# Eight VectorE lo parts a block: five to an accumulating DMA, three tiles to whole fp32 matmuls

## The reference, cut to what matters

```python
e = stack([tbl_f[ids[:, f]] for f in range(39)])          # (1024, 39, 16), x0
xk = x0
for idx, (W, b) in enumerate(params):                     # W: (39, fields of xk, 128)
    z = relu(einsum('bhd,bkd,hks->bsd', x0, xk, W) + b)
    xk, direct = z[:, :64], z[:, 64:]                     # the last layer: all of z is direct
logit = sum(concatenate(direct, axis=1), axis=-1)
h = relu(concat([logit, dense_ctx]) @ W_top1 + b_top1)
h = relu(h @ W_top2 + b_top2)
y = h @ W_top3
```

## Time and profile before

| | |
|---|---|
| median of 3 runs | 1450.75 us (1449.77 to 1451.19) |
| the profiled execution's own time | 1451.21 us |
| its span, first to last instruction | 1449.1 us |
| mean granted TensorE clock | 0.991 |
| VectorE busy | 1325.9 us, 92% |
| TensorE busy (ends modelled) | 1262.3 us, 87% |
| GpSimd busy | 1233.7 us, 85% |
| ScalarE busy | 638.6 us, 44% |
| DMA: read from HBM, written | 193.17 MB, 12.78 MB |

### The profile page before, as it was taken

How to read it: one execution, slowest core, us unless ns; L and a number is a source line. 1 busy time by engine, 2 the same in 40 slices (tenths; PEclk the granted TensorE clock), 3 DMA queues, 4 the chain that set the end, 5 groups by cost and what they waited for, 6 DMA issues and landing times.

```text
span 1449.1 us, 15741 instructions
## 1 busy us (share of the span) xinstructions
PE 1262.3 (87%) x4040; PEld 730.6 (50%) x4040; DVE 1325.9 (92%) x959; ACT 638.6 (44%) x640; POOL 1233.7 (85%) x655
## 2 busy tenths in 40 slices
PE   0378989999898999989899998989999898999899
PEld 0244545545454555545455554545555554655555
DVE  1389999999999999999999999999999999999872
ACT  1135434454544435454453545444453535535443
POOL 6788989899898989989898998989899896857571
PEclk9989999999999999999999999999999999999999
DMA  4852708154270906327090633618062351806000
GB/s 108 292 178 55 275 6 289 37 198 132 69 260 7 314 10 205 125 79 250 13 313 5 225 105 93 236 25 304 2 228 102 122 206 33 293 1 220 0 0 1
DMA packets 81243, 196.26 MB, mean 135 GB/s; under 512 B 23983, under 2 KB 35342, under 8 KB 81193
## 3 DMA queue, kind: packets, MB, share of 16 engines
q1 hardware_dynamic: 70953, 193.14, 38.8%
q0 software_dynamic: 10240, 2.64, 1.7%
HBM read 193.17 MB, written 12.78 MB: 142 GB/s over the span
## 4 chain that ended last, share of the span: by engine, by line
POOL 58%; issue 22%; PE 10%; DVE 6%; DMA 1%; ACT 1%; POOLq 0%; SPq 0%; DVEq 0%; ACTq 0%
POOL lo L453 29%; POOL emb L443 28%; PE acc L819 8%; DVE prod L716 4%; DVE lo L729 1%; POOL block_idx L432 1%; ACT hi L585 1%; DVE logit L764 0%; POOL pairs_r L473 0%; DMA x_tiles<-x_rows 0%; DVE hi L726 0%; DMA x_rows<-x_rows 0%; PE xk L873 0%; PE acc L873 0%; PE acc L900 0%
## 5 line engine op out<-in xcount | busy, mean ns | idle before, releaser
L453 POOL TENSOR_TENSOR lo<-prod,hi 128x1024 fp32r<-128x1024 f32 (+1 forms) x304 | 758.4, 2500 | 117.0 <-ACT hi L585 113.3
L585 ACT ACTIVATE hi<-prod 128x1024 fp32r<-128x1024 f32 (+1 forms) x464 | 488.1, 1058 | 729.2 <-DVE prod L716 628.4
L716 DVE TENSOR_TENSOR prod<-x_tiles,xk 128x1024 f32<-128x1024 f32 x640 | 740.7, 1212 | 49.2 <-PE acc L819 30.3
L819 PE MATMUL acc<-prod,wfull 128*128 128x512 f32 (+2 forms) x1152 | 549.4, 600 | 1.1 <-DVE prod L716 0.9
L443 POOL DMA_INDIRECT emb<-table,block_idx x320 | 444.3, 1389 | 67.2 <-issue 60.9
L819 PE MATMUL acc<-lo,whi 128*128 128x512 f32 (+1 forms) x864 | 329.7, 466 | 112.8 <-POOL lo L453 92.9
L819 PE MATMUL acc<-hi,whi 128*128 128x512 f32 (+1 forms) x928 | 384.8, 420 | 32.6 <-ACT hi L585 32.4
L819 PE MATMUL acc<-hi,wlo 128*128 128x512 f32 (+2 forms) x928 | 364.7, 398 | 0.0
L819 PEld LDWEIGHTS acc<-lo,whi 128*128 128x128 f32 (+1 forms) x864 | 145.6, 189 | 323.0 <-POOL lo L453 245.8
L819 PEld LDWEIGHTS acc<-prod,wfull 128*128 128x128 f32 (+2 forms) x1152 | 219.9, 191 | 168.5 <-issue 141.3
L729 DVE TENSOR_TENSOR lo<-prod,hi 128x1024 fp32r<-128x1024 f32 (+1 forms) x128 | 276.5, 2160 | 1.1 <-ACT hi L585 1.1
(11 more groups left out here) (62 smaller groups left out, 129.6 us busy)
## 6 DMA issues: line engine op xcount, KB each, us to landing
x_tiles<-x_rows SPq DMA_DIRECT2D x304, 512.0 KB, 9.4
x_rows<-x_rows SPq DMA_DIRECT2D x16, 624.0 KB
x_tiles<-x_rows SPq DMA_DIRECT2D x32, 256.0 KB, 10.4
x_stack<-x_rows SPq DMA_DIRECT2D x48, 156.0 KB
emb<-table,block_idx POOLq DMA_INDIRECT x320, 3.4
x_rows<-x0T SPq DMA_DIRECT2D x64, 32.0 KB, 1.5
x_tiles<-w SPq DMA_DIRECT2D x1, 832.0 KB, 9.3
x_tiles<-w SPq DMA_DIRECT2D x1, 768.0 KB, 6.4
```

What stands on the lines that cost most here:

```text
L453: nc.gpsimd.tensor_tensor(lo[0:r, product_slot(j), :], prod[0:r, product_slot(j), :], hi[0:r, part_slot(j), :].bitcast(f32), ALU.subtract) ...
L585: nc.scalar.activation(hi[0:r, part_slot(j), :], prod[0:r, product_slot(j), :], ACT.Copy).then_inc(hi_ready, 1)
L716: nc.vector.tensor_tensor(prod[0:r, product_slot(j), :], in0, in1, ALU.mult).then_inc(product_ready, 1)
L819: mm = nc.tensor.matmul(z[:, c], w[0:r], part[0:r, c], start=first and i == 0, stop=last and i == len(weights) - 1)
```

## The change

`KINDS` has no D any more. In layer 0 both D tiles become F; in layer 1 the last one does; the other five, tiles 2 and 7 of layer 1 and 2, 7 and 17 of layer 2, become a new kind A. An A tile's lo part isn't subtracted by an engine. ScalarE copies the product a second time, times -1 and rounded, into one of two slots of a new tile `negative`. GpSimd issues a DMA that adds the product from `prod` onto it. TensorE waits for that DMA's own semaphore and multiplies `negative` as the lo part. GpSimd's list has the A tiles among its G tiles, so the gathers are spread over 10, 12 and 2 places. The order of tiles, the slots of products and the loads stay. To make room, `base_sb`, used at the start only, lies where `x0_stack` is.

```diff
-KINDS = ["GFDGDFF", "GFDGF" * 2 + "GFHGF" + "GFDGF", "GGDGF" + "GFDGF" + "GFHGF" + "GFDGF"]
+KINDS = ["GFFGFFF", "GFAGF" * 2 + "GFHGF" + "GFFGF", "GGAGF" + "GFAGF" + "GFHGF" + "GFAGF"]
...
-PRODS, PARTS = 6, 4
+PRODS, PARTS, NEGATIVES = 6, 4, 2
...
+SUMMED = [j for j, k in enumerate(KIND) if k == "A"]
+def negative_slot(j):
+    return SUMMED.index(j) % NEGATIVES
+def negative_before(n, j):
+    return next(i for i in earlier(n, j) if i <= -6 or KIND[i] == "A" and negative_slot(i % STEP) == negative_slot(j))
...
-        base_sb = sb("base_sb", [128, BLOCKS * PAIRS], i32)
+        negative = sb("negative", [128, NEGATIVES, COLS], f32r)
+        base_sb = nc.alloc_sbuf_tensor_at("base_sb", [128, BLOCKS * PAIRS], i32, offset=stack_at)
+        negative_ready = sem("negative_ready")
+        lo_summed = [sem(f"lo_summed{a}") for a in range(len(SUMMED))]
...
GpSimd:
+            def sum_lo(n, j):
+                pool.wait_ge(negative_ready, reached(n, j, "A"))
+                pool.nop(nofuse=True)
+                pool.dma_start(out=negative[:, negative_slot(j), :], in_=prod[:, product_slot(j), :],
+                               accum_op=ALU.add).then_inc(lo_summed[SUMMED.index(j)], 16)
...
-                at, tiles = (L0, L1, L2)[l], [t for t, k in enumerate(KINDS[l]) if k == "G"]
+                at, tiles = (L0, L1, L2)[l], [t for t, k in enumerate(KINDS[l]) if k in "GA"]
...
-                    subtract(n, at + t)
+                    if KINDS[l][t] == "G":
+                        subtract(n, at + t)
+                    else:
+                        sum_lo(n, at + t)
...
ScalarE, in round_hi, behind the hi part:
+                        if KIND[j] == "A":
+                            act.wait_ge(tile_used, reached(n, negative_before(n, j), "FDGHA"))
+                            nc.scalar.activation(negative[:, negative_slot(j), :], prod[:, product_slot(j), :],
+                                                 ACT.Copy, scale=-1.0).then_inc(negative_ready, 1)
...
TensorE, in lo_part:
-                    if KIND[j] in "DH":
+                    if KIND[j] == "A":
+                        part = negative[:, negative_slot(j), :]
+                        pe.wait_ge(lo_summed[SUMMED.index(j)], 16 * (n + 1))
+                    elif KIND[j] in "DH":
```

More of the change, by code:

```diff
@@ L81 @@
 KIND = [KINDS[l][t] for l, t in ORDER]
+SUMMED = [j for j, k in enumerate(KIND) if k == "A"]
+assert not any(L0 <= j < L2 for j in SUMMED)
 def rows(l, t):
@@ L398, in step @@
                     for t in range(REST):
-                        sp.wait_ge(product_ready, reached(n, L2 + t, "FDGH"))
+                        sp.wait_ge(product_ready, reached(n, L2 + t, "FDGHA"))
                         sp.nop(nofuse=True)
@@ L413, in step @@
                 elif not past_end(n, 1):
-                    sp.wait_ge(product_ready, reached(n, STEP - 1, "FDGH"))
+                    sp.wait_ge(product_ready, reached(n, STEP - 1, "FDGHA"))
                     load_top()
@@ L580, in round_hi @@
                         r = rows(*ORDER[j])
-                        act.wait_ge(product_ready, reached(n, j, "FDGH"))
+                        act.wait_ge(product_ready, reached(n, j, "FDGHA"))
                         if not is_step(n, PROLOGUE) or SPLITS[0].index(ORDER[j][1]) >= PARTS:
-                            act.wait_ge(tile_used, reached(n, parts_before(n, j), "FDGH"))
+                            act.wait_ge(tile_used, reached(n, parts_before(n, j), "FDGHA"))
                         nc.scalar.activation(hi[0:r, part_slot(j), :], prod[0:r, product_slot(j), :],
                                              ACT.Copy).then_inc(hi_ready, 1)
+                        if KIND[j] == "A":
+                            act.wait_ge(tile_used, reached(n, negative_before(n, j), "FDGHA"))
+                            nc.scalar.activation(negative[:, negative_slot(j), :], prod[:, product_slot(j), :],
+                                                 ACT.Copy, scale=-1.0).then_inc(negative_ready, 1)
             def round_top():
@@ L650, in step @@
                     round_hi(n, L1 + Z2_AFTER, L0)
-                    evacuate(1, n, z1, reached(n, L0 - 1, "FDGH"))
+                    evacuate(1, n, z1, reached(n, L0 - 1, "FDGHA"))
                     evacuate_direct1(z1)
@@ L661, in step @@
                         round_hi(n, L2 + TOP1_AFTER + 2 * m, min(STEP, L2 + TOP1_AFTER + 2 * m + 2))
-                    evacuate(2, n, z2, reached(n, STEP - 1, "FDGH"))
+                    evacuate(2, n, z2, reached(n, STEP - 1, "FDGHA"))
                     return
                 round_hi(n, L1 + Z2_AFTER, L0 + XK1_AFTER)
-                evacuate(1, n, z1, reached(n, L0 - 1, "FDGH"), copied=2)
+                evacuate(1, n, z1, reached(n, L0 - 1, "FDGHA"), copied=2)
                 round_hi(n, L0 + XK1_AFTER, L0 + DIRECT1_AFTER)
@@ L671, in step @@
                 round_hi(n, L0 + COPY_AFTER, L2 + Z0_AFTER)
-                evacuate(0, n + 1, z0, reached(n, L2 - 1, "FDGH"), copied=None if past_end(n, 2) else n + 3)
+                evacuate(0, n + 1, z0, reached(n, L2 - 1, "FDGHA"), copied=None if past_end(n, 2) else n + 3)
                 round_hi(n, L2 + Z0_AFTER, STEP)
                 round_hi(n + 1, L1, L1 + Z2_AFTER)
-                evacuate(2, n, z2, reached(n, STEP - 1, "FDGH"))
+                evacuate(2, n, z2, reached(n, STEP - 1, "FDGHA"))
             each_step(act, step)
@@ L711, in product @@
                 if not is_step(n, PROLOGUE) or j - L0 >= PRODS:
-                    dve.wait_ge(tile_used, reached(n, product_before(n, j), "FDGH"))
+                    dve.wait_ge(tile_used, reached(n, product_before(n, j), "FDGHA"))
                 tile = x0_tiles[0:r, tile_slot(1 - parity if l == 0 else parity, TILES[l][t]), :]
@@ L720, in subtract @@
                 r = rows(*ORDER[j])
-                dve.wait_ge(hi_ready, reached(n, j, "DGH"))
+                dve.wait_ge(hi_ready, reached(n, j, "DGHA"))
                 if KIND[j] == "H":
@@ L842, in contract @@
                         w = FULL_AT[l] + FULLS[l].index(t)
-                        pe.wait_ge(product_ready, reached(n, j, "FDGH"))
+                        pe.wait_ge(product_ready, reached(n, j, "FDGHA"))
                         mm = multiply(j, [wfull[:, w, :]], prod[:, product_slot(j), :], j == start, j == stop - 1)
@@ L851, in contract @@
                         w = SPLIT_AT[l] + SPLITS[l].index(t)
-                        pe.wait_ge(hi_ready, reached(n, j, "DGH"))
+                        pe.wait_ge(hi_ready, reached(n, j, "DGHA"))
                         if KIND[j] == "H":
```

2 lines of the change are left out of this document (1 added, 1 removed).

## The result

The changed kernel takes 1638.65 us (median of 4 runs, 1637.09 to 1639.93) against 1450.78: a ratio of 1.130, 95% interval 1.128 to 1.132. The forecast was 1435, its range ended at 1512. The profiled execution's span is 1638.0 us, its mean granted clock 0.925 (0.991 before).

The account below looks back on a forecast made before the run. GpSimd's queue was taken to bound 83.95 us blocks, VectorE close behind. New block: 75.9 + 1.1 + 1.6 + 4.0 + 0.5 = 83.1; 13 x -0.85 = -11, then -3 and -2, gave 1435 us, range 1400 to 1512.

Parts of the forecast that it names:

- C: Rival, chance 0.12: GpSimd's DMA issue is dearer, 2 us instead of 0.96; 86.6 us a block, 1486 us.
- quiet L: Time from a sum's issue to its landing away from the tile loads: 2.5 + 2.6 = 5.1 us.
- busy L: Time from a sum's issue to its landing in layer 2's burst of tile loads: 6.3 + 2.5 = 8.8 us.
- E: Rival, chance 0.07: the accumulating transfer is slow in itself, over 8 us quiet; all five stop the queue, over 1520 us.
- Against L + 3.3 stands GpSimd's own queue: Landing time plus 3.3 us to the subtract, set against GpSimd's work since the issue: needs 8.4 quiet, 12.1 in burst.
- I followed the releases: Product slot releases traced from layer 1's first sum: 1.1 us idle at subtract 18, 1.6 before layer 0.
- 7.2 us of idle a block: GpSimd's idle beside its 75.9 us queue: 1.1 + 1.6 + 4.0 + 0.5.
- taken up: Layer 2's tile 17 is 0.7 us late, absorbed by the idle in front of subtract 18.
- 4.0 us idle forecast at one subtract: Layer 2's tile 7: GpSimd has 8.1 us of work, the sum needs 12.1, so it idles before subtract 13.
- A: Rival, chance 0.24: layer 2's tile 7 sum gets half the engines in the burst, landing in 11.4 us; 87 us a block, 1491.
- 9.4: Landing time in us in the burst from which the block is again 83.95 us and the slower rival decides.
- A granted clock well under 0.99: Listed among the signs that would show the forecast wrong; no time was attached to it.

Follow-up runs that it names:

- experiment 2: Changed kernel with 24 zero-weight passes on TensorE ahead of its wait at layer 2's tiles 2 and 17: 1648.01 us, ratio 1.136.
- e1: Changed kernel whose DMAs add a constant weight tile onto one unread slot; TensorE multiplies the hi part without waiting (sums not the reference's): 1445.19 us, ratio 0.998.
- e14: Changed kernel with hi, product and negated slots listed so that none comes back early at the turn from layer 2 to layer 1: 1618.33 us, ratio 1.116.
- e3: Changed kernel with all five A tiles back as VectorE subtracts, only the three F tiles kept: 1362.79 us, ratio 0.940.
- e5: Changed kernel with A tiles in layer 1 only, layer 2's three back as VectorE subtracts, three F kept: 1425.26 us, ratio 0.982.

## Why the prediction was wrong

**What held.** The engine totals: VectorE 68.9 us a block (65 forecast). The issue: 0.99 to 1.01 us against 0.96, so C's premise was false. The gathers: 1.46 to 1.16 us in the mean, those beside no subtract of VectorE 0.96 to 1.06; the two beside H stay at 1.77. The landings: 4.7 and 4.8 us in layer 1 (quiet L 5.1), and 8.8 at layer 2's tile 17 (busy L 8.8). At tile 7 the landing was later than forecast: 9.2 to 10.5 us where TensorE waits for it, 8.8 to 10.1 in experiment 2. So E came out by its number and not by its mechanism: the sum is not slow in itself. Layer 2's tile 2 was put ahead of the burst and lies in it (7.1 us in the median); that alone cost 1 us idle.

The rule of the Trainium skill (SBUF — State Buffer, "Who interferes with whom") by which gathers would stay at 1.46 is contradicted again, and the measurement decides: 1135 ns in the mean instead of 1389 once the subtracts are gone.

**What failed** is the step "Against L + 3.3 stands GpSimd's own queue", with "I followed the releases": the overlap of the landings with GpSimd's queue, counted at 7.2 us of idle a block, was 15.9. The intervals on GpSimd between events of a block are medians over the blocks that start between 400 and 1200 us; the forecast's are its own terms put in order (they sum to 82.7 of its 83.1):

| from, to | forecast | after | e1, no wait |
|---|---|---|---|
| index copy, layer 2 tile 2 | 19.1 | 19.5 | 20.6 |
| tile 2, tile 7 | 8.1 | 8.2 | 8.2 |
| tile 7, tile 17 | 18.5 | 23.0 | 15.0 |
| tile 17, layer 1 tile 2 | 9.2 | 14.8 | 11.0 |
| layer 1 tile 2, tile 7 | 9.2 | 9.5 | 9.4 |
| layer 1 tile 7, index copy | 18.6 | 22.0 | 18.4 |

Of e1's 11.0 some 1.6 us are that experiment's own wait; its queue there is the 9.4 of e14. The forecast counted one subtract as late and the ones behind it as on time. It missed at three places.

*The turn, +5.6.* Tile 17's lateness of 0.7 us was to be "taken up". I counted six tiles and four split tiles on from it inside a layer. Across the turn the slot counts don't divide: layer 1's first hi part stands in tile 17's slot, two split tiles on. GpSimd idles 5.22 us at 759.11. e14 removes the early return and brings the interval to 9.4 us (forecast 9.2). So the early return is shown as what holds GpSimd at this place; as a price it is worth only 2.0 us of the block, since the rest is lost again at the next sum.

*Behind tile 7, +4.5.* The 4.0 us idle forecast at one subtract, with 0.5 at tile 17, came as 1.02, 2.94, 0.77, 1.58 and 1.39, in all 7.7. The landing sets most of it: without the wait for it the interval is 15.0 us (experiment 1), and TensorE stands in front of tile 7's sum in seven of nine blocks. The 1.58 stands behind H: VectorE, no longer ahead of GpSimd, does H's subtract directly in front of the product that GpSimd needs next, and meets GpSimd in it (2.41 us at 739.39, 3.94 at 781.07; an uncontended full one takes 1.22). Its mean rose from 1810 to 2818 ns; in e3, without sums, it is 1699, and in e5, with the two quiet sums alone, already 2769. How the 4.5 us divide between landing and H was not separated; the run that would do it, H's tiles as F beside the five sums, was not made. Nor was one with layer 2's sums moved out of the loads' stretch.

*The end of layer 1, +3.4.* Before layer 0, the same 1.58 behind H, and a last subtract of 3.34 instead of 2.4. This, the four contended gathers and gaps of 0.30 between two DMAs instead of 0.16 are also most of the queue's +4.9 us: subtracts 47.2 for 46.1 (where the earlier trace rows themselves sum to 46.4), gathers, issues and gaps 32.4 for 28.3.

The forecast gave sums the cover of GpSimd's queue as if VectorE and TensorE came to each sum with their slack restored. They don't: each landing stops TensorE in order, six products later VectorE, then ScalarE, then GpSimd, and the kernel has five of these in 96 us.

**The rivals.** A named the right place, layer 2 in the burst, and priced it at 6.6 us idle there by L = 11.4; L was 9.2 to 10.5 and the idle 7.7. Its own threshold, 9.4, was passed in most blocks. But with A's longer landing the same working gave 1491 us, 148 short of the result: the size of L is the smaller error, the count of what follows each landing the larger. "A granted clock well under 0.99" was listed as a sign of being wrong, and it fell to 0.925; it is a consequence of the waits and, by experiment 2, not their price. Not priced by any case: the three F alone. They gain 6% (gathers at 1188 ns in e3 for 1389, some 4 of its 5.9 us a block, with nothing added on GpSimd); the working took this gain and charged it to the queue in one sum, and so did not see that the other half of the edit loses by itself.

## What to carry to other kernels

A transfer put into an in-order chain is covered only if every engine behind it has slack at that moment: count slots across the turn of the loop, and follow each landing until the slack is back, before crediting another engine's queue as cover. Where an edit has two halves, sum each alone: here one was worth -88 us, the other +276. When a wait has taken the clock down, restore the clock before blaming it: here that was worth nothing that the time shows.

## What the runs showed of the hardware

An accumulating DMA of 512 KB from SBUF to SBUF costs GpSimd 0.99 us to issue, a plain one 0.59. It lands in 4.7 us in quiet stretches and in 6.4 to 10.5 beside the tile loads. With half the bytes the issue takes the same 1.01 us (median) and the landing 3.5 in quiet; a plain copy of 512 KB lands in 3.0. The forecast's way to 5.1 (a gather's 2.7 less waiting, and twice the bytes at the bursts' rate) was near for the sum. A gather directly behind a sum waits 0.30 us and takes 1.05, behind another gather 0.30 and 0.95, behind a subtract 0.16 and 0.96.

TensorE's granted clock was at half (1.2 GHz) from 720 to 730 us, after the engine had stood in a wait since 717.8; at that level an F tile took 3.62 us instead of 1.88. The window, then TensorE's timeline of the changed kernel:

```profile
720.00:730.00 10.00, 4.89 (x8) 2.54 (x9) 1.22 (x1) 1.67 (x2) 8.52 (x6) 0.50 1.01 305
```

```profile
726.13 3.62 PE L848 MATMUL acc<-prod,wfull 128*128 128x512 f32 x4
```
